# Window attention on one core: the bias of V moved to ScalarE, the image change cut anew, and TensorE's turn and spread set before the first row scores

## The chip, the cores and the metric

The kernel runs on one core of a Trainium2 chip. The time is that of the device, in microseconds, median over runs. The profile shows five engines: TensorE (PE, with its weight loads as PEld), VectorE (DVE), ScalarE (ACT), GpSimd (POOL) and SyncE (SP), which here only issues DMAs.

## The reference

The input x is 4 images of 128 channels, 112 by 112 pixels, float32. Each image is normalised in 32 groups of 4 channels, shifted by 3 pixels, projected to Q, K and V, cut into 256 windows of 7 by 7 pixels, and each window gets attention in 8 heads of 16 channels. The result is shifted back and added to x:

```python
y = group_norm(x, groups=32, eps=1e-5)
qkv = einsum('bchw,oc->bohw', roll(y, (-3, -3)), w_qkv) + b_qkv
# per window of 49 tokens and head of 16 channels:
attn = softmax(q @ k.T / sqrt(16)); o = attn @ v
out = x + roll(windows_back(o), (3, 3))
```

## The kernel before

Every engine has an instruction stream of its own, written out by hand, and semaphores tie them together. An image is 16 bands of 7 rows, a band is two groups of 8 windows (the second one wraps around the right edge, so its pixels are reached in three pieces instead of one), and the 4 images give 128 groups. Every engine has a function `step(g, ...)`, and in step g it works on several groups at once: the projections of g+1, the row scores of g, the column scores and exponentials of g-1, and sums, output and inverse of g-2. The groups are software pipelined, the order within a step is the order of the calls.

**TensorE**, step g: `project_v(g)` (L725), `sum_keys(g-2)` (L783), `weigh(g-2)` (L797), `project_q(g+1)` (L716), `row_scores(g, 0)` (L740), `turn_max(g-1)` (L752), `spread_inverse(g-2)` (L808), `column_scores(g-1)` (L765, and L772 for the part that subtracts the maximum), `row_scores(g, 1)` (L740), `project_k(g+1)` (L709). Row scores are only there to find each row's maximum. The turn transposes the negated maxima, the spread copies the inverse sums to all rows. `weigh` and `column_scores` share PSUM banks 6 and 7; turn, spread and V share bank 5.

**ScalarE**, step g: `evac_k(g)` (L356), `normalise(g+2)` (L349, `xn`, one or three pieces), `high_inverse(g-2)` (L384, `inv_hi`), `evac_even(g-2)` (L390, `even_out`), `evac_v(g)` (L379, `v_rows`), `evac_q(g+1)` (L361), `evac_neg(g-1)` (L368), two `exp(g-1)` (L373, `probs_t`).

**VectorE**, step g: `mask_q(g)` (L564), statistics of the next image in chunks of 448 pixels (L487, 28 chunks per image), `invert(g-2)` (L576, a reciprocal) and `low_inverse(g-2)` (L581), `join(g-2)` (L588, `summed`), `maximum(g, 0)` (L571), `low_q(g+1)` (L556), `scale_rows(g-2)` (L597, `mixed`), `maximum(g, 1)`. The join waits for `even_out`, and `column_scores` waits for the join. `change_image(b)` runs 6 steps, at b*32-8 to b*32-3, in which the statistics chunk is left out and the mean, variance and inverse root of the next image are worked out in small instructions, some ahead of `invert` and some between `low_inverse` and `join`. A Newton step for the root is L537 to L539; `gather_channels` is L507.

**POOL**, step g: `add_bias(g-3)` (L291), `split_max(g-1)`, `split_k(g)`, `add_image(g-3)` (L300, into `stage`), `split_x(g+2)`.

**SyncE** stores each band when both of its groups are in `stage`, and then loads the same band of the image after the next into the slot just freed (`load_band`, L201 and L202). So bands of images 2 and 3 arrive one by one while images 0 and 1 are stored. VectorE waits for them ahead of its statistics:

```python
for n in range(3):
    dve.wait_ge(loaded[b + 1], 32 * -(-(2 * n + 2) * STAT // BAND))
    two_steps(first + n, 2 * n, at)
dve.wait_ge(loaded[b + 1], 32 * BANDS)
```

Here `first` is b*16-1, so these are steps 30 to 35 for b = 1 and the last wait, for all 16 bands, stands ahead of step 36. The next two steps have two chunks each.

Of the kernel before, what the change touches and what calls it, by code (L numbers as in the profile page):

```python
# [6 lines left out]
B, C, H, W = 4, 128, 112, 112  # L7
# [5 lines left out]
BANDS = H // WS  # L13
# [22 lines left out]
def window_attention(nc, x, w_qkv, b_qkv, out):  # L36
# [7 lines left out]
    with ctx:  # L44
# [181 lines left out]
        def _(pool):  # L226
# [61 lines left out]
            def add_bias(g, half):  # L288
                pool.wait_ge(mixed_done, g + 2)
                pool.sem_inc(waited, 1)  # L290
                nc.gpsimd.tensor_scalar(mixed[:, half, :, :], mixed[:, half, :, :], bias[:, 2:3], None, ALU.add).then_inc(bias_added, 1)  # L291

# [12 lines left out]
            def step(g, n, par):  # L305
                if live(g - 3):
                    add_bias(g - 3, 1 - par)
                if live(g - 1):
                    split_max(g - 1, 1 - par)
                if live(g):  # L310
                    split_k(g, par)
                if live(g - 3):
                    add_image(g - 3, n - 2 + par, 1 - par)
                if live(g + 2):
                    split_x(g + 2, par)
# [12 lines left out]
        def _(act):  # L328
# [23 lines left out]

            def evac_k(g):
                act.wait_ge(k_mm, g + 1)
                wait(act, k_split, g)
                nc.scalar.activation(k32[:, :], psum[:, QK_BANK, 0:GT], ACT.Identity, bias=k_bias[:, 0:1]).then_inc(k_evac, 1)  # L356
# [35 lines left out]
            def step(g, n, par, b=0):  # L392
                if live(g):
                    evac_k(g)
                if live(g + 2):
                    normalise(g + 2, n + 1, par, b)
                if live(g - 2):
                    high_inverse(g - 2)
                if live(g - 2):
                    evac_even(g - 2)  # L400
                if live(g):
                    evac_v(g, par)
                if live(g + 1):
                    evac_q(g + 1)
                if live(g - 1):
                    evac_neg(g - 1)
                if live(g - 1):
                    exp(g - 1, 0)
                    exp(g - 1, 1)
# [14 lines left out]
            for g in range(GROUPS - 2, GROUPS + 2):  # L424
                step(g, g // 2, g & 1)

        @block.vector
        def _(dve):
# [87 lines left out]
            def group_mean():  # L516

                link(nc.vector.tensor_reduce(g_sum[:, :], grouped(mean_row), AX.X, ALU.add))
                link(nc.vector.scalar_tensor_tensor(grouped(work_a), g_sum[:, :, None].broadcast_to([C, 8, PER]), -1.0 / PER,
                                                    grouped(mean_row), ALU.mult, ALU.add))  # L520
                link(nc.vector.tensor_tensor(work_b[:, :], work_a[:, :], work_a[:, :], ALU.mult))

            def group_variance():

                link(nc.vector.tensor_tensor(work_a[:, :], work_b[:, :], var_row[:, :], ALU.add))
                link(nc.vector.tensor_reduce(g_var[:, :], grouped(work_a), AX.X, ALU.add))
                link(nc.vector.tensor_scalar(g_var[:, :], g_var[:, :], 1.0 / PER, EPS, ALU.mult, ALU.add))

            def guess_root():

                link(nc.vector.tensor_scalar(half_bits[:, :], g_var[:, :].bitcast(i32), 1, None, ALU.logical_shift_right))
                link(nc.vector.tensor_scalar(rs[:, :].bitcast(i32), half_bits[:, :], -1.0, float(0x5F3759DF), ALU.mult, ALU.add))

            def refine_root(steps):

                for _ in range(steps):
                    link(nc.vector.tensor_tensor(rs_t[:, :], rs[:, :], rs[:, :], ALU.mult))  # L537
                    link(nc.vector.scalar_tensor_tensor(rs_t[:, :], rs_t[:, :], -0.5, g_var[:, :], ALU.mult, ALU.mult))
                    link(nc.vector.scalar_tensor_tensor(rs[:, :], rs_t[:, :], 1.5, rs[:, :], ALU.add, ALU.mult))  # L539

            def scatter_groups():

                nc.vector.tensor_scalar(grouped(mean_row), g_sum[:, :, None].broadcast_to([C, 8, PER]), 1.0 / PER, None, ALU.mult)
                link(nc.vector.tensor_scalar(grouped(var_row), rs[:, :, None].broadcast_to([C, 8, PER]), X_SCALE, None, ALU.mult))

            def offer(b):

                wait(dve, xn_ready, (b - 1) * 2 * BANDS)
                nc.vector.transpose(mean_c[:, :], mean_row[:, :])
                link(nc.vector.transpose(rstd_c[:, b % 2, :], var_row[:, :]))  # L550
                nc.vector.scalar_tensor_tensor(shift_c[:, b % 2:b % 2 + 1], mean_c[:, 0:1], -1.0, rstd_c[:, b % 2, 0:1], ALU.mult,  # L551
                                               ALU.mult).then_inc(norm_ready, 1)

# [47 lines left out]
            def step(g, n, par, chunks=(), image_at=None, ahead=None, between=None):  # L601
# [11 lines left out]
                if between:  # L613
                    between()
# [16 lines left out]
            def change_image(b):  # L631

                g = (b * BANDS - 4) * 2
                for ahead, between in ((None, lambda: gather_channels(b)),
                                       (turn_channels, group_mean),
                                       (group_variance, guess_root),
                                       (lambda: refine_root(1), lambda: refine_root(1)),
                                       (lambda: refine_root(NEWTON - 2), scatter_groups),
                                       (None, lambda: offer(b))):
                    step(g, g // 2, g & 1, ahead=ahead, between=between)  # L640
                    g += 1
# [9 lines left out]
            gather_channels(0)  # L651
            turn_channels()
            group_mean()
            group_variance()
            guess_root()
            refine_root(NEWTON)
            scatter_groups()
            offer(0)
# [5 lines left out]
            step(2, 1, 0)  # L664
            step(3, 1, 1)
            with dve.Fori(2, BANDS - 4) as n:
                two_steps(n, 2 * n + 4, BANDS * BAND)
            for b in (1, 2):
# [3 lines left out]
                for n in range(3):  # L672
# [3 lines left out]
                for g in (2 * first + 6, 2 * first + 7):  # L676
                    chunk = 6 + 2 * (g & 1)
                    step(g, g // 2, g & 1, (chunk, chunk + 1), at)
                with dve.Fori(4, CHUNKS // 2 - 1) as n:
                    two_steps(n + first, 2 * n + 2, at)  # L680
# [10 lines left out]
        def _(pe):  # L691
# [120 lines left out]
            def step(g, par):  # L812
# [9 lines left out]
                if live(g):  # L822
                    row_scores(g, par, 0)
                if live(g - 1):
                    turn_max(g - 1, live(g))
                if live(g - 2):
                    spread_inverse(g - 2)
                if live(g - 1):
# [34 lines left out]
```

## Time and profile before

| | |
|---|---|
| median of 3 runs | 943.32 us (942.41 to 944.63) |
| the profiled execution | 941.08 us, its span 938.9 us |
| TensorE busy | 865.0 us, 92% of the span |
| VectorE busy | 766.3 us, 82% |
| POOL busy | 739.3 us, 79% |
| ScalarE busy | 665.1 us, 71% |
| mean granted TensorE clock | 0.99 |
| one ordinary step | 6.69 us |

Times are counted from the start of the span. A row of the timeline gives start, duration, engine, line, operation and tiles; "x3" behind it means three instructions of one kind merged; a bracket says how long the engine was idle before it and who ended that. Consecutive instructions of ScalarE and VectorE overlap a little, so the pitch from start to start can be shorter than the duration.

### The profile page before, as it was taken

The page shows a single profiled execution, that of the slowest core. Times are in us where ns is not written, and L with a number is a line of the kernel's source. Part 1 is how long each engine was busy: PE and PEld are TensorE (multiplying, and loading weights), DVE is VectorE, ACT ScalarE, POOL GpSimd, SP SyncE. Part 2 cuts the span into 40 slices and gives each one's busy share as a digit, 9 for nine tenths or more (in the row PEclk, how much of TensorE's full clock was granted, in tenths as well). Part 3 has the DMA queues.
Part 4 walks back from the last instruction along what each step waited for, and adds up shares of the span by engine and source line. Part 5 has one row for each costly group of instructions (what it writes and reads, how often), then busy time and mean ns, then how long its engine had stood idle before and what let it go on. Part 6 is the DMA issues. An engine that isn't in the chain of part 4 may idle for free. (4 is left out here: it accounts for less than half of the span.)

```text
span 938.9 us, 104445 instructions
## 1 busy us (share of the span) xinstructions
PE 865.0 (92%) x46473; PEld 708.7 (75%) x46473; DVE 766.3 (82%) x1399; ACT 665.1 (71%) x1297; POOL 739.3 (79%) x1191
## 2 busy tenths in 40 slices
PE   0479999998999999999999999999899999999994
PEld 0358888887788888887788888887678888888883
DVE  8657888889889888888888888888987777777873
ACT  2347777776677777777677777777677777777772
POOL 1347888887788888888788888888788888888883
PEclk9999999999999999999999999999999999999998
DMA  9401122112112211221211000000000000000001
GB/s 380 177 5 58 46 68 68 60 42 69 48 55 68 69 43 60 68 68 34 69 54 50 35 34 34 17 34 34 17 34 35 19 32 34 34 22 29 34 34 36
DMA packets 29912, 51.87 MB, mean 55 GB/s; under 512 B 3649, under 2 KB 28865, under 8 KB 29761
## 3 DMA queue, kind: packets, MB, share of 16 engines
q1 hardware_dynamic: 29888, 51.59, 15.8%
q8 instruction: 11, 0.18, 0.1%
q14 instruction: 13, 0.10, 0.0%
HBM read 25.89 MB, written 25.69 MB: 55 GB/s over the span
## 5 line engine op out<-in xcount | busy, mean ns | idle before, releaser
L373 ACT ACTIVATE probs_t<-psum,exp_scale 128x800 f32<-128x800 f32 x256 | 223.2, 923 | 139.6 <-PE psum L772 139.6
L571 DVE TENSOR_REDUCE neg_max<-psum 100x16 f32<-100x784 f32 x256 | 249.2, 974 | 39.1 <-PE psum L740 31.1
L291 POOL TENSOR_SCALAR mixed<-mixed,bias 128x392 f32<-128x392 f32 x128 | 161.7, 1263 | 123.2 <-DVE mixed L597 123.2
L740 PEld LDWEIGHTS psum<-k_hi,q_masks 32*128 32x128 f16 x8192 | 175.3, 91 | 46.3 <-issue 42.8
L740 PE MATMUL psum<-k_hi,q_masks 32*128 32x49 f16 x8192 | 197.8, 179 | 3.0 <-DVE neg_max L571 2.3
L740 PE MATMUL psum<-k_lo,q_masks 32*128 32x49 f16 x4096 | 182.6, 179 | 0.0
L740 PEld LDWEIGHTS psum<-k_lo,q_masks 32*128 32x128 f16 x4096 | 161.0, 91 | 0.0
L300 POOL TENSOR_TENSOR stage<-mixed,image 128x343 f32 (+7 forms) x256 | 144.2, 583 | 0.4 <-POOL mixed L291 0.4
L765 PE MATMUL psum<-q_masks,k_hi 32*64 32x100 f16 x8192 | 128.7, 219 | 16.1 <-DVE summed L588 13.3
L349 ACT ACTIVATE xn<-image,shift_c,rstd_c 128x21 f32 (+6 forms) x256 | 132.4, 573 | 8.0 <-DVE shift_c L551 6.1
L797 PE MATMUL psum<-probs_t,v_rows 64*32 64x100 f32 x8192 | 131.4, 252 | 2.4 <-issue 2.4
L783 PE MATMUL psum<-probs_t,sum_rows 128*32 128x49 f32 x8192 | 117.7, 209 | 9.6 <-ACT probs_t L373 2.7
L783 PEld LDWEIGHTS psum<-probs_t,sum_rows 128*32 128x32 f32 x8192 | 103.8, 110 | 28.5 <-issue 25.2
L275 POOL TENSOR_TENSOR k_lo<-k,k_hi 128x392 f16<-128x392 f32 x128 | 116.5, 910 | 10.7
L265 POOL TENSOR_TENSOR xn_lo<-xn,xn_hi 128x392 f16<-128x392 f32 x128 | 116.2, 908 | 10.7
L564 DVE TENSOR_SCALAR q_masks<-q_halves,even_odd 128x800 f16<-128x800 f16 x256 | 120.6, 511 | 2.3 <-DMA image<-in_x_dram 2.3
L765 PEld LDWEIGHTS psum<-q_masks,k_hi 32*64 32x64 f16 x8192 | 103.5, 102 | 22.5 <-issue 17.8
L765 PE MATMUL psum<-q_masks,k_lo 32*64 32x100 f16 x4096 | 111.7, 218 | 0.0
L797 PEld LDWEIGHTS psum<-probs_t,v_rows 64*32 64x32 f32 x8192 | 102.5, 106 | 11.4 <-issue 2.8
L588 DVE SCALAR_TENSOR_TENSOR summed<-psum,v_scale,even_out 128x392 f32<-128x392 f32 x128 | 80.1, 625 | 38.1 <-ACT even_out L390 37.4
L725 PE MATMUL psum<-w_lo,xn_hi 128*128 128x128 f16 x512 | 94.9, 222 | 0.0
L725 PE MATMUL psum<-w_hi,xn_lo 128*128 128x128 f16 x512 | 94.8, 222 | 0.0
(112 smaller groups left out, 1828.2 us busy)
## 6 DMA issues: line engine op xcount, KB each, us to landing
out_dram<-stage SPq DMA_DIRECT2D x64, 224.0 KB, 2.1
out_dram<-stage SPq DMA_DIRECT2D x64, 168.0 KB, 1.9
image<-in_x_dram SPq DMA_DIRECT2D x32, 224.0 KB, 2.6
image<-in_x_dram SPq DMA_DIRECT2D x1, 6104.0 KB, 28.2
image<-in_x_dram SPq DMA_DIRECT2D x34, 168.0 KB, 2.5
image<-in_x_dram SPq DMA_DIRECT2D x6, 896.0 KB, 9.2
image<-in_x_dram SPq DMA_DIRECT2D x1, 728.0 KB, 14.3
w_nat<-in_L_conv_w_qkv_dram SPq DMA_DIRECT2D x1, 192.0 KB, 2.4
```

What stands on the lines that cost most here:

```text
L275: nc.gpsimd.tensor_tensor(k_lo[:, par, :, 0:TOK], k, k_hi[:, par, :, 0:TOK], ALU.subtract).then_inc(k_split, 1)
L291: nc.gpsimd.tensor_scalar(mixed[:, half, :, :], mixed[:, half, :, :], bias[:, 2:3], None, ALU.add).then_inc(bias_added, 1)
L300: last = nc.gpsimd.tensor_tensor(pixel_view(stage[:, bass.ds(st, BAND)], piece), token_view(mixed[:, half, :, :], piece), pixel_view(image ...
L349: last = nc.scalar.activation(token_view(xn, piece), pixel_view(image[:, bass.ds(at, BAND)], piece), ACT.Identity, bias=shift_c[:, b % 2:b ...
L373: nc.scalar.activation(probs_t[:, 2 * u:2 * u + 2, :, :].rearrange("p h a q -> p h (a q)"), psum[:, COL_BANKS[u], 0:PAIRS * ROWS2], ACT.Ex ...
L564: last = nc.vector.tensor_scalar(both[:, :, e, :], q_halves[:, :, :, :].rearrange("p l w q -> p (l w) q"), even_odd[:, e:e + 1], None, ALU ...
L571: nc.vector.tensor_reduce(neg_max[:, par, 2 * j:2 * j + 2, :], psum[0:ROWS2, ROW_BANKS, 0:GT] .rearrange("p h (w k) -> p h w k", k=TOK), A ...
L725: last = nc.tensor.matmul(psum[:, V_BANK, a * C:(a + 1) * C], xs[:, par, 2 * a:2 * a + 2, :].rearrange("p w k -> p (w k)"), wv[:, 2, :], s ...
L740: last = nc.tensor.matmul(psum[:, ROW_BANKS.start + h - 2 * j, w * TOK:(w + 1) * TOK], q_masks[rows, par, low + w * ROWS2:low + w * ROWS2 ...
L765: nc.tensor.matmul(psum[side, COL_BANKS[h // 2].start + h % 2, a * ROWS2:(a + 1) * ROWS2], k[rows, par, w, :], q_masks[rows, par, low + w ...
L783: last = nc.tensor.matmul(psum[c * PC:(c + 1) * PC, SUM_BANK, SPARE_SUM], sum_rows[:, a, e, :, :, :].rearrange("p t w s -> p (t w s)"), pr ...
L797: last = nc.tensor.matmul(psum[c * PC:(c + 1) * PC, OUT_BANKS.start + s, a * C:a * C + ROWS2], v_rows[side, par, a, c * PC:(c + 1) * PC], ...
```

## The change

Four edits go together. `add_bias` leaves POOL and becomes an activation on ScalarE, behind `normalise` and ahead of `high_inverse`; ScalarE's last loop gets one step more for it. On ScalarE `evac_v` now stands before `evac_even`. VectorE's image change becomes a list of pieces, one per step and each ahead of `invert` (with three Newton steps it is eight entries), it starts two steps earlier, and the chunks of statistics are dealt out anew: steps 2 and 3 get one each, the steps behind an image change have two chunks from the third pair on, and the wait for all bands stands ahead of that third pair. TensorE issues `turn_max` and `spread_inverse` before `row_scores(g, par, 0)`.

```diff
@@ gpsimd
-            def add_bias(g, half):
-                pool.wait_ge(mixed_done, g + 2)
-                pool.sem_inc(waited, 1)
-                nc.gpsimd.tensor_scalar(mixed[:, half, :, :], mixed[:, half, :, :], bias[:, 2:3], None, ALU.add).then_inc(bias_added, 1)
...
             def step(g, n, par):
-                if live(g - 3):
-                    add_bias(g - 3, 1 - par)
@@ scalar
+            def add_bias(g, half):
+                act.wait_ge(mixed_done, g + 2)
+                nc.scalar.activation(mixed[:, half, :, :], mixed[:, half, :, :], ACT.Identity, bias=bias[:, 2:3]).then_inc(bias_added, 1)
...
                     normalise(g + 2, n + 1, par, b)
+                if live(g - 3):
+                    add_bias(g - 3, 1 - par)
                 if live(g - 2):
                     high_inverse(g - 2)
+                if live(g):
+                    evac_v(g, par)
                 if live(g - 2):
                     evac_even(g - 2)
-                if live(g):
-                    evac_v(g, par)
...
-            for g in range(GROUPS - 2, GROUPS + 2):
+            for g in range(GROUPS - 2, GROUPS + 3):
@@ vector
+            def norm_steps(b):
+                return [lambda: gather_channels(b), turn_channels, group_mean, group_variance] + NEWTON * [refine_root] + [lambda: offer(b)]
...
             def change_image(b):
-                g = (b * BANDS - 4) * 2
-                for ahead, between in ((None, lambda: gather_channels(b)),
-                                       (turn_channels, group_mean),
-                                       (group_variance, guess_root),
-                                       (lambda: refine_root(1), lambda: refine_root(1)),
-                                       (lambda: refine_root(NEWTON - 2), scatter_groups),
-                                       (None, lambda: offer(b))):
-                    step(g, g // 2, g & 1, ahead=ahead, between=between)
-                    g += 1
+                first = (b * BANDS - 5) * 2
+                for g, piece in enumerate(norm_steps(b), first):
+                    step(g, g // 2, g & 1, ahead=piece)
...
-            step(2, 1, 0)
-            step(3, 1, 1)
-            with dve.Fori(2, BANDS - 4) as n:
-                two_steps(n, 2 * n + 4, BANDS * BAND)
+            step(2, 1, 0, (8,), BANDS * BAND)
+            step(3, 1, 1, (9,), BANDS * BAND)
+            with dve.Fori(2, BANDS - 5) as n:
+                two_steps(n, 2 * n + 6, BANDS * BAND)
...
-                for n in range(3):
+                for n in range(2):
                     dve.wait_ge(loaded[b + 1], 32 * -(-(2 * n + 2) * STAT // BAND))
                     two_steps(first + n, 2 * n, at)
                 dve.wait_ge(loaded[b + 1], 32 * BANDS)
-                for g in (2 * first + 6, 2 * first + 7):
-                    chunk = 6 + 2 * (g & 1)
-                    step(g, g // 2, g & 1, (chunk, chunk + 1), at)
-                with dve.Fori(4, CHUNKS // 2 - 1) as n:
-                    two_steps(n + first, 2 * n + 2, at)
+                for n in (2, 3):
+                    for par in range(2):
+                        chunk = 4 * (n - 1) + 2 * par
+                        step(2 * (first + n) + par, first + n, par, (chunk, chunk + 1), at)
+                with dve.Fori(4, CHUNKS // 2 - 2) as n:
+                    two_steps(n + first, 2 * n + 4, at)
@@ tensor
                     project_q(g + 1, 1 - par)
-                if live(g):
-                    row_scores(g, par, 0)
                 if live(g - 1):
                     turn_max(g - 1, live(g))
                 if live(g - 2):
                     spread_inverse(g - 2)
+                if live(g):
+                    row_scores(g, par, 0)
                 if live(g - 1):
                     column_scores(g - 1, 1 - par)
```

The addition of variance and squared deviation moves from `group_variance` into `group_mean`, the first guess of the root from a function of its own into `group_variance`, and `scatter_groups` into `offer`. The instructions themselves are the same.

## Rows read from the trace of the kernel before

**Rows 1.** The page's first part: busy time, share and instructions of the engines.

```profile
PE 865.0 (92%) x46473; PEld 708.7 (75%) x46473; DVE 766.3 (82%) x1399; ACT 665.1 (71%) x1297; POOL 739.3 (79%) x1191
```

**Rows 2.** The timeline of ScalarE in an odd step (start, us, engine, line).

```profile
504.50 1.74 ACT L373 ACTIVATE probs_t<-psum,exp_scale 128x800 f32<-128x800 f32 x2 [0.95 <-PE psum L772]
...
506.60 1.31 ACT L349 ACTIVATE xn<-image,shift_c,rstd_c 128x343 f32 x3
507.86 0.24 ACT L384 CAST inv_hi<-inv 128x49 f16<-128x49 f32 x1
508.28 0.59 ACT L390 ACTIVATE even_out<-psum,v_scale 128x392 f32<-128x392 f32 x1 [0.19 <-PE psum L797]
508.77 0.58 ACT L379 COPY v_rows<-psum 128x512 f32<-128x512 f32 x1
...
511.19 1.74 ACT L373 ACTIVATE probs_t<-psum,exp_scale 128x800 f32<-128x800 f32 x2 [0.95 <-PE psum L772]
```

**Rows 3.** The timeline of VectorE: a join, masks of step 34, a late join.

```profile
508.90 0.63 DVE L588 SCALAR_TENSOR_TENSOR summed<-psum,v_scale,even_out 128x392 f32<-128x392 f32 x1 [0.32 <-ACT even_out L390]
...
278.93 0.95 DVE L564 TENSOR_SCALAR q_masks<-q_halves,even_odd 128x800 f16<-128x800 f16 x2
...
241.58 0.63 DVE L588 SCALAR_TENSOR_TENSOR summed<-psum,v_scale,even_out 128x392 f32<-128x392 f32 x1
```

**Rows 4.** The timeline of TensorE from Q to the column scores.

```profile
501.84 0.33 PE L716 MATMUL psum<-xn_hi,w_lo 128*128 128x392 f16 x1
...
502.10 0.20 PE L740 MATMUL psum<-k_hi,q_masks 32*128 32x49 f16 x2
...
502.81 0.22 PE L752 MATMUL psum<-ident,neg_halves 100*128 100x100 bf16 x1
...
503.15 0.25 PE L765 MATMUL psum<-q_masks,k_hi 32*64 32x100 f16 x8
...
242.35 0.25 PE L765 MATMUL psum<-q_masks,k_hi 32*64 32x100 f16 x8 [0.40 <-DVE summed L588]
```

**Rows 5.** The page's costliest groups: busy and mean ns, idle before, its releaser.

```profile
L291 POOL TENSOR_SCALAR mixed<-mixed,bias 128x392 f32<-128x392 f32 x128 | 161.7, 1263 | 123.2 <-DVE mixed L597 123.2
```

**Rows 6.** The timeline of ScalarE in an even step, step 34.

```profile
277.45 1.74 ACT L373 ACTIVATE probs_t<-psum,exp_scale 128x800 f32<-128x800 f32 x2 [0.95 <-PE psum L772]
...
279.56 0.75 ACT L349 ACTIVATE xn<-image,shift_c,rstd_c 128x392 f32 x1
280.90 0.24 ACT L384 CAST inv_hi<-inv 128x49 f16<-128x49 f32 x1 [0.59 <-DVE inv L576]
```

**Rows 7.** The timeline of ScalarE in a step with two chunks.

```profile
515.15 0.24 ACT L384 CAST inv_hi<-inv 128x49 f16<-128x49 f32 x1 [1.10 <-DVE inv L576]
515.29 0.58 ACT L390 ACTIVATE even_out<-psum,v_scale 128x392 f32<-128x392 f32 x1
...
518.17 1.74 ACT L373 ACTIVATE probs_t<-psum,exp_scale 128x800 f32<-128x800 f32 x2 [0.95 <-PE psum L772]
```

**Rows 8.** ScalarE's timeline: exponentials at both ends of an image change.

```profile
205.64 1.75 ACT L373 ACTIVATE probs_t<-psum,exp_scale 128x800 f32<-128x800 f32 x2 [0.95 <-PE psum L772]
...
250.69 1.74 ACT L373 ACTIVATE probs_t<-psum,exp_scale 128x800 f32<-128x800 f32 x2 [1.26 <-PE psum L772]
```

**Rows 9.** VectorE's timeline: first instruction of a Newton step and its follower.

```profile
230.11 0.20 DVE L537 TENSOR_TENSOR rs_t<-rs 128x8 f32<-128x8 f32 x1
...
231.03 0.47 DVE L576 RECIPROCAL inv<-psum 128x49 f32<-128x49 f32 x1
```

**Rows 10.** SyncE's timeline: the last part of image 2's last band.

```profile
284.96 0.35 SPq L202 DMA_DIRECT2D image<-in_x_dram  x1
```

**Rows 11.** Line L202 alone: time from its DMAs to their landing.

```profile
DMA to landing us min/median/max: 2.4/2.5/3.1
```

**Rows 12.** The windows view: busy times, granted clock, DMA, behind a change's waits.

```profile
455.60:459.10 3.50, 3.50 (x90) 2.82 (x79) 2.88 (x8) 2.77 (x4) 2.14 (x4) 0.54 0.01 2
```

More of the change, by code:

```diff
@@ L521, in group_mean, with refine_root, offer @@
                 link(nc.vector.tensor_tensor(work_b[:, :], work_a[:, :], work_a[:, :], ALU.mult))
+                link(nc.vector.tensor_tensor(work_a[:, :], work_b[:, :], var_row[:, :], ALU.add))
             def group_variance():
-                link(nc.vector.tensor_tensor(work_a[:, :], work_b[:, :], var_row[:, :], ALU.add))
                 link(nc.vector.tensor_reduce(g_var[:, :], grouped(work_a), AX.X, ALU.add))
                 link(nc.vector.tensor_scalar(g_var[:, :], g_var[:, :], 1.0 / PER, EPS, ALU.mult, ALU.add))
-            def guess_root():
                 link(nc.vector.tensor_scalar(half_bits[:, :], g_var[:, :].bitcast(i32), 1, None, ALU.logical_shift_right))
                 link(nc.vector.tensor_scalar(rs[:, :].bitcast(i32), half_bits[:, :], -1.0, float(0x5F3759DF), ALU.mult, ALU.add))
[L534 to L541, printed above, removed]
+            def refine_root():
+                link(nc.vector.tensor_tensor(rs_t[:, :], rs[:, :], rs[:, :], ALU.mult))
+                link(nc.vector.scalar_tensor_tensor(rs_t[:, :], rs_t[:, :], -0.5, g_var[:, :], ALU.mult, ALU.mult))
+                link(nc.vector.scalar_tensor_tensor(rs[:, :], rs_t[:, :], 1.5, rs[:, :], ALU.add, ALU.mult))
+            def offer(b):
+                wait(dve, xn_ready, (b - 1) * 2 * BANDS)
                 nc.vector.tensor_scalar(grouped(mean_row), g_sum[:, :, None].broadcast_to([C, 8, PER]), 1.0 / PER, None, ALU.mult)
                 link(nc.vector.tensor_scalar(grouped(var_row), rs[:, :, None].broadcast_to([C, 8, PER]), X_SCALE, None, ALU.mult))
-            def offer(b):
-                wait(dve, xn_ready, (b - 1) * 2 * BANDS)
                 nc.vector.transpose(mean_c[:, :], mean_row[:, :])
@@ L599, in scale_rows, with step @@
                                         summed[:, :, :].rearrange("p (s a) q -> p s a q", s=2), ALU.mult).then_inc(mixed_done, 1)
-            def step(g, n, par, chunks=(), image_at=None, ahead=None, between=None):
+            def step(g, n, par, chunks=(), image_at=None, ahead=None):
                 if live(g):
@@ L612, in step @@
                     low_inverse(g - 2)
-                if between:
-                    between()
                 if live(g - 2):
@@ L650, in _ @@
                     take_stats(chunk * STAT, chunk)
[L651 to L658, printed above, removed]
+            for piece in norm_steps(0):
+                piece()
             work_out_scales()
```

## The prediction

> **What bounds the kernel now.** I read the busy line of the page first. TensorE is busy for 92% of the span [rows 1], and no other engine is above 82%, so a change on another engine counts only where TensorE waits for it. Then I laid the timelines of ScalarE, VectorE and TensorE for one step beside each other. From one first exponential (the start of `exp(g-1, 0)`) to the next is 504.50 to 511.19, so 6.69 us a step [rows 2]. I call the start of that first exponential T and give all other moments as T plus so much, because the chain goes round in it: the exponentials feed `sum_keys` and `weigh` of the next step, behind these come Q, the row scores and the column scores, and the column scores release the next exponential.
>
> In an odd step ScalarE starts `xn` at T+2.10, `inv_hi` at T+3.36, `even_out` at T+3.78 and `v_rows` at T+4.27 [rows 2]. VectorE starts the join (L588) at T+4.40 [rows 3]. `column_scores` waits for that join, since `weigh` left its result in banks 6 and 7. How tight is it? Where the join does come last, it ends at 241.58 + 0.63 = 242.21 and the column scores start at 242.35 [rows 3, 4], a lag of 0.14. From the start of the column scores to the next exponential is 503.15 to 504.50 = 1.35 [rows 2, 4]. So a join that starts at J allows the next exponential at J + 0.63 + 0.14 + 1.35 = J + 2.12. Now J is T+4.40, which allows T+6.52, and the step takes 6.69: the slack is 0.17 us. That number decides most of what follows.
>
> **The change part by part.**
>
> TensorE order. Now there are three changes of matmul shape between Q and the column scores: Q (128x128) to row scores (32x128), row scores to turn and spread (128x128), these to the column scores (32x64). The first costs 0.10: the last Q matmul starts at 501.84, streams its 392 columns in about 0.16 (its neighbours' pitch is 0.17), and the row scores start at 502.10 [rows 4]. After it there are two: Q and turn share a shape. One gap of 0.09 to 0.10 goes, and I take 0.09 of each of 128 steps, 11.5 us at the very most, if nothing else waits. The trace of before has no direct step from 32x128 to 32x64; if that were free, the saving would be 0.19 a step. The Trainium skill, TensorEngine Tiling (Array Packing), Key Properties, says that changing the tiling mode drains TensorE; by it one of three drains goes, and the gap of 0.10 agrees.
>
> What is paid: `turn_max` waits for `v_rows` of this step. From the turn to the next exponential is then 0.34 (turn, spread and a gap: 502.81 to 503.15), 0.71 (row scores and a gap: 502.10 to 502.81) and 1.35: 2.40 [rows 2, 4].
>
> ScalarE. POOL loses an instruction of 1.263 us [rows 5], but POOL idles before it and its first reader waits for nothing of it, so that saves nothing on the path. ScalarE gains an activation over 392 columns. It has no such one from SBUF with a bias alone; the nearest rows are `even_out`, 0.59 long and 0.49 in pitch to the next [rows 2], and `xn` in one piece, 0.75 [rows 6], a pitch of about 0.64. I take 0.49 and keep 0.64 for the range. It stands ahead of `inv_hi`, and behind it `v_rows` now goes ahead of `even_out`, another 0.49. `inv_hi` to its successor is 0.14 when that is ready [rows 7]; `even_out` to the join is 0.62 [rows 2, 3].
>
> - Odd step (three pieces of `xn`): `inv_hi` T+3.36+0.49 = 3.85, `v_rows` 3.99, `even_out` 4.48, join 5.10, next exponential 7.22. Against 6.69 that is +0.53. The turn's own chain gives less: `v_rows` ends at 4.57, turn about 4.67, plus 2.40 = 7.07.
> - Even step: `xn` starts at T+2.11 in one piece of 0.75 [rows 6], so the bias fits before `inv_hi`, which waits for the reciprocal until T+3.45 (277.45 to 280.90). `v_rows` 3.59, `even_out` 4.08, join 4.70, next exponential 6.82: +0.13.
>
> Mean +0.33. This holds with one chunk of statistics in the step or none (odd steps are ScalarE's in both). Ordinary steps: 4 to 21, 30 to 33 and 38 to 53, 62 to 65 and 70 to 85, and the last image, 34 less the drain of the pipeline: about 90. 90 x 0.33 = 29.7 us.
>
> Steps with two chunks. There `inv_hi` comes at 515.15 - 511.19 = T+3.96, and the step takes 6.98 to the exponential at 518.17 [rows 2, 7]. After: 3.96 + 0.14 + 0.49 + 0.62 + 2.12 = 7.33. The change makes four of them per image (34 to 37) out of two. Leaving the first aside: 3 x 7.33 - (6.69 + 2 x 6.98) = +1.3, for two images +2.6.
>
> The image change. Six steps take 205.64 to 250.69 = 45.05 [rows 8], with the two ordinary ones that the eight pieces now also use, 58.43. A piece now stands ahead of the reciprocal and takes the place of a chunk of about 0.54, with nothing between inverse and join. A Newton step takes 230.11 to 231.03 = 0.92 [rows 9], so `inv_hi` at 3.45 + 0.38 = 3.83 and the step 7.20; the odd floor is 7.22. The two widest pieces (aggregate, and the mean with an addition more) I put at 7.2 and 7.7. Eight steps then sum to about 58.3. That is a gain over the old 7.5 us a step, given back by the two steps more and by ScalarE: 0 us, with 2 either way per image.
>
> The wait for the next image, moved by the same edit. Two-step pairs 15 and 16 (steps 30 to 33) now come before `dve.wait_ge(loaded[b+1], 32 * BANDS)`, not three pairs, so VectorE meets it at the start of step 34 (and 66). But band 15 of image b+1 is only loaded after band 15 of image b-1 is stored, and that one is finished by POOL's `add_image(31)` inside step 34. The second half of that load is issued at 284.96 [rows 10]. T of that step is 277.45 and VectorE starts its masks at 278.93 = T+1.48 [rows 3, 6]. So the issue is at T+7.51, and the landing takes 2.5 us at the median [rows 11]. POOL without the bias is some 0.2 earlier, so VectorE goes on at about T+9.8, not T+1.48: it stands for 8.3 us. Today it meets the wait at step 36, 13.4 later, when all has landed. Queued behind it are masks, statistics, reciprocal, join and both maxima. From masks to `inv_hi` in a two-chunk step is 3.96 - 1.48 = 2.48, and from `inv_hi` to the exponential 3.37, so the next T is 9.8 + 5.85 = 15.65, +8.96 over 6.69. Nothing covers it: TensorE stops at the turn. Twice: 17.9 us. POOL and SyncE need nothing of VectorE's step 34 for that store and load, so it is a stall and not a deadlock.
>
> The clock. Behind the waits of the second image change the granted clock was 0.54 over 3.5 us [rows 12]. That is 1.2 GHz of its two levels nearly throughout. TensorE idle for almost 9 us should bring the same: a stretch of 3.4 us at half rate costs at most 1.7, two cost 3.4, and partly covered one next to nothing. I take 1.5 per stall, 3 in all. The Trainium skill, TensorE: Matmul & The Clock Gate, Part 1, has the clock halved after idleness; without any such fall the sum would be 3 us less.
>
> Sum: 29.7 + 2.6 + 0 + 17.9 + 3 = 53.2. The profiled execution took 941.1, so 994.3; it lies 2.2 under the median of the runs shown, 943.3, so **996 us**.
>
> **The rivals.**
>
> - A, the forecast: ScalarE's chain and the load wait both bind. 996.
> - B, only the load wait binds: the bias and the swap hide in ScalarE's idle time (0.95 us before the exponentials [rows 2]). Against: that idle time lies behind the join, not ahead of it. 943.3 + 17.9 + 3 + 2.6, less up to 8 for the gap saved in 90 steps: 959 to 967.
> - C, only ScalarE's chain binds, since the loads are in time. Against: the issue at 284.96 stands 6.0 behind the masks. 943.3 + 29.7 + 2.6 = 976.
> - D, faster: the gap saved decides. It does if `even_out` still starts by T+3.95 (3.78 + 0.17) and `v_rows` ends before Q does, T+4.2, and the load costs under the saving. 0.09 x 128 = 11.5: 932; with the second gap free too, 920. Against: both conditions are missed in odd steps by 0.5 and 0.4.
> - E, worse: the bias has a pitch of 0.64 (+0.15 in 45 odd steps, 7), the clock stays down longer (to 3.4 per stall, 4 more), the mean piece is slowed by POOL. 1003 to 1012.
>
> **How the numbers follow.** A 0.72, B 0.08, C 0.06, D 0.03, E 0.09, and 0.02 for cancelling terms that leave no change. A alone spans 984 to 1003 (mean step +0.25 to +0.38, clock 0 to 6). Leaving out D, part of B and the top of E gives 966 to 1008. Within 0.2% is about what a measurement of this kernel cannot tell from no change: faster 0.03, same 0.02, slower 0.95.
>
> **What would show it.** Ordinary steps that alternate near 6.8 and 7.2 instead of 6.69; TensorE waiting ahead of L752 for `v_rows` or ahead of the column scores for the join in nearly every odd step; ScalarE idle less than 0.95 before the exponentials only if I am wrong on what is late. Two waits of VectorE's masks for the image load of about 8 us, at steps 34 and 66, and the granted clock down behind each. Eight change steps of 7.2 to 7.7 with none near 8.6. I am wrong if steps stay at 6.6 to 6.7 (then the bias was covered), or if VectorE passes the load wait without stopping.

## The result and the profile after

The changed kernel takes **1001.07 us** (median of 4 runs, 1000.26 to 1001.44), against 943.39 for the kernel before in the same series: a ratio of 1.0609, interval 1.0591 to 1.0628. It is 6% slower; the prediction was 996, in a range of 966 to 1008. The profiled span grew from 938.9 to 998.5 us. The page's first part and one of its costliest groups:

```profile
PE 883.4 (88%) x46473; PEld 716.9 (72%) x46473; DVE 732.6 (73%) x1399; ACT 706.9 (71%) x1425; POOL 600.3 (60%) x1063
...
L559 DVE TENSOR_SCALAR q_masks<-q_halves,even_odd 128x800 f16<-128x800 f16 x256 | 97.7, 424 | 19.1 <-DMA image<-in_x_dram 19.1
```

Against [rows 1] POOL lost 139 us and ScalarE gained 42, yet TensorE's share fell to 88%. VectorE's masks (L559) now wait 19.1 us for the image load. The rest of the loss is in no single wait. Cut at the first exponentials of the steps, the 59.6 us are:

| stretch | before | after less before | predicted |
|---|---|---|---|
| 89 ordinary steps | 595.6 | +36.8 | +29.4 |
| steps 34, 35, 66, 67 | 26.8 | +23.2 | +22.2 |
| steps 36, 37, 68, 69 | 28.0 | +1.4 | +1.4 |
| three image changes, 27 steps | 196.2 | -3.2 | 0 |
| head, steps 2 to 4, end | 92.3 | +1.4 | 0 |

An odd step takes 7.16 to 7.17 us and an even one 7.06, in place of 6.69 for both. ScalarE's timeline, an even step and then an odd one:

```profile
497.96 1.74 ACT L370 ACTIVATE probs_t<-psum,exp_scale 128x800 f32<-128x800 f32 x2 [1.54 <-PE psum L754]
...
500.06 0.76 ACT L342 ACTIVATE xn<-image,shift_c,rstd_c 128x392 f32 x1
500.70 0.63 ACT L348 ACTIVATE mixed<-mixed,bias 128x392 f32<-128x392 f32 x1
501.39 0.24 ACT L381 CAST inv_hi<-inv 128x49 f16<-128x49 f32 x1
501.80 0.58 ACT L376 COPY v_rows<-psum 128x512 f32<-128x512 f32 x1 [0.17 <-PE psum L779]
502.28 0.59 ACT L387 ACTIVATE even_out<-psum,v_scale 128x392 f32<-128x392 f32 x1
...
505.01 1.74 ACT L370 ACTIVATE probs_t<-psum,exp_scale 128x800 f32<-128x800 f32 x2 [1.53 <-PE psum L754]
506.65 0.59 ACT L353 ACTIVATE k<-psum,k_bias 128x392 f32<-128x392 f32 x1
507.12 1.32 ACT L342 ACTIVATE xn<-image,shift_c,rstd_c 128x343 f32 x3
508.32 0.62 ACT L348 ACTIVATE mixed<-mixed,bias 128x392 f32<-128x392 f32 x1
508.83 0.23 ACT L381 CAST inv_hi<-inv 128x49 f16<-128x49 f32 x1
508.96 0.59 ACT L376 COPY v_rows<-psum 128x512 f32<-128x512 f32 x1
509.43 0.60 ACT L387 ACTIVATE even_out<-psum,v_scale 128x392 f32<-128x392 f32 x1
...
512.18 0.93 ACT L370 ACTIVATE probs_t<-psum,exp_scale 128x800 f32<-128x800 f32 x1 [1.54 <-PE psum L754]
```

In the odd step nothing between `xn` and `even_out` waits: it is one queue, and `even_out` starts at T+4.42 where it was T+3.78 [rows 2]. In the even step there is one wait, that of `v_rows` for L779, which is `weigh`: after its `inv_hi` there are 0.41 us to `v_rows` and not 0.13. That wait is the prediction's gap (below). ScalarE's idle time before the exponentials rose from 0.95 to 1.5, so its own load is not what is short; the place of each instruction in the queue is.

The joins that close both steps, and the turn of the even one (VectorE's and TensorE's timelines):

```profile
502.90 0.62 DVE L583 SCALAR_TENSOR_TENSOR summed<-psum,v_scale,even_out 128x392 f32<-128x392 f32 x1 [0.74 <-ACT even_out L387]
...
510.07 0.63 DVE L583 SCALAR_TENSOR_TENSOR summed<-psum,v_scale,even_out 128x392 f32<-128x392 f32 x1 [0.69 <-ACT even_out L387]
```

```profile
502.52 0.20 PE L734 MATMUL psum<-ident,neg_halves 100*128 100x100 bf16 x1 [0.21 <-ACT v_rows L376]
...
502.86 0.20 PE L722 MATMUL psum<-k_hi,q_masks 32*128 32x49 f16 x2
...
503.68 0.25 PE L747 MATMUL psum<-q_masks,k_hi 32*64 32x100 f16 x8
```

Join plus 2.12 gives 505.02 and 512.19; the exponentials start at 505.01 and 512.18. So the constant taken from before holds. The turn waits for `v_rows` in every step but one, as forecast, and row scores follow it by 0.34. From row scores to column scores are then 0.82 us, where 0.71 is enough [rows 4]: the column scores stand about 0.1 for the join, which ends at 503.52, 0.16 before they start. So the join sets the step, and the turn's chain would be ready 0.1 earlier. The profile names the join as what the column scores wait for in one step alone of this kernel; what bears the reading out is `c_swap_only` (below), where a join at the same T+4.95 gives the same step of 7.06 and the profile names it in 126 steps.

Step 34, VectorE and ScalarE, and the windows view around it (us, busy time and instructions by engine, granted clock, DMA share, GB/s):

```profile
287.82 0.97 DVE L566 TENSOR_REDUCE neg_max<-psum 100x16 f32<-100x784 f32 x1
297.23 0.77 DVE L559 TENSOR_SCALAR q_masks<-q_halves,even_odd 128x800 f16<-128x800 f16 x2 [8.44 <-DMA image<-in_x_dram]
```

```profile
287.23 1.74 ACT L370 ACTIVATE probs_t<-psum,exp_scale 128x800 f32<-128x800 f32 x2 [1.54 <-PE psum L754]
...
299.54 0.24 ACT L381 CAST inv_hi<-inv 128x49 f16<-128x49 f32 x1 [8.94 <-DVE inv L571]
...
303.76 1.75 ACT L370 ACTIVATE probs_t<-psum,exp_scale 128x800 f32<-128x800 f32 x2 [2.41 <-PE psum L754]
```

```profile
278.00:292.00 14.00, 13.09 (x717) 10.61 (x717) 8.97 (x15) 9.52 (x19) 9.10 (x17) 1.00 0.18 57
292.00:307.00 15.00, 6.60 (x232) 5.61 (x232) 7.33 (x15) 4.72 (x10) 2.84 (x8) 0.55 0.16 54
307.00:320.00 13.00, 12.15 (x700) 9.89 (x701) 10.61 (x18) 8.62 (x20) 8.31 (x14) 0.99 0.08 27
```

The masks wait 8.44 us, until T+10.00 (T+9.8 predicted); the step takes 16.53 and the next 8.46. The granted clock, 1.00 before, is 0.55 over the next 15 us, nearly all at 1.2 GHz, and comes back after that.

### The profile page after: what moved, and what is told of

It reads as the page before. It is cut to its first block, busy times and chain, and to the rows that moved or that the text cites. A ratio compares the mean times of both kernels' runs of the same rounds, so it can differ in the third digit from the quotient of the medians.

```text
span 998.5 us, 104360 instructions
## 1 busy us (share of the span) xinstructions
PE 883.4 (88%) x46473; PEld 716.9 (72%) x46473; DVE 732.6 (73%) x1399; ACT 706.9 (71%) x1425; POOL 600.3 (60%) x1063
## 4 chain that ended last, share of the span: by engine, by line
PE 53%; ACT 22%; issue 14%; DVE 5%; DMA 3%; ACTq 1%; SPq 1%; POOL 0%; POOLq 0%; DVEq 0%
PE psum L722 13%; PE psum L747 12%; ACT xn L342 8%; ACT v_rows L376 7%; PE psum L779 6%; PE psum L765 5%; PE psum L707 4%; PE psum L691 4%; PE psum L754 4%; DMA image<-in_x_dram 3%; ACT probs_t L370 3%; PE psum L790 3%; PE psum L734 3%; ACT mixed L348 2%; ACT k L353 1%
## 5 line engine op out<-in xcount | busy, mean ns | idle before, releaser
L282 POOL TENSOR_SCALAR neg_halves<-neg_max 100x32 bf16<-100x32 f32 x128 | 61.9, 483 | 297.9 <-DVE neg_max L566 297.9
L779 PE MATMUL psum<-probs_t,v_rows 64*32 64x100 f32 x8192 | 131.1, 252 | 2.0 <-issue 2.0
L765 PE MATMUL psum<-probs_t,sum_rows 128*32 128x49 f32 x8192 | 117.8, 209 | 10.3 <-ACT probs_t L370 2.7
L747 PEld LDWEIGHTS psum<-q_masks,k_hi 32*64 32x64 f16 x8192 | 107.5, 103 | 17.9 <-issue 3.3
L747 PE MATMUL psum<-q_masks,k_lo 32*64 32x100 f16 x4096 | 114.5, 219 | 0.0
L559 DVE TENSOR_SCALAR q_masks<-q_halves,even_odd 128x800 f16<-128x800 f16 x256 | 97.7, 424 | 19.1 <-DMA image<-in_x_dram 19.1
L779 PEld LDWEIGHTS psum<-probs_t,v_rows 64*32 64x32 f32 x8192 | 102.4, 106 | 10.9 <-issue 2.3
L576 DVE SCALAR_TENSOR_TENSOR inv_rows<-inv_hi,low_rows,inv 128x49 f16<-128x49 f16 x128 | 49.1, 384 | 70.6 <-ACT inv_hi L381 70.6
```

Of the source, the lines that this page charges most:

```text
L559: last = nc.vector.tensor_scalar(both[:, :, e, :], q_halves[:, :, :, :].rearrange("p l w q -> p (l w) q"), even_odd[:, e:e + 1], None, ALU ...
L747: nc.tensor.matmul(psum[side, COL_BANKS[h // 2].start + h % 2, a * ROWS2:(a + 1) * ROWS2], k[rows, par, w, :], q_masks[rows, par, low + w ...
L765: last = nc.tensor.matmul(psum[c * PC:(c + 1) * PC, SUM_BANK, SPARE_SUM], sum_rows[:, a, e, :, :, :].rearrange("p t w s -> p (t w s)"), pr ...
L779: last = nc.tensor.matmul(psum[c * PC:(c + 1) * PC, OUT_BANKS.start + s, a * C:a * C + ROWS2], v_rows[side, par, a, c * PC:(c + 1) * PC], ...
```

## The experiments

Each was compared with the kernel before on the same chip (medians 941.1 to 941.7). Step times are from first exponential to first exponential, and the columns "ordinary", "34/35, 66/67" and "changes" below are the rows of the table above: the difference from the kernel before, summed, in us.

### The load wait, and the order on ScalarE

`a_load_in_time` is the changed kernel with that wait where it costs nothing:

```diff
-                dve.wait_ge(loaded[b + 1], 32 * BANDS)
                 for n in (2, 3):
                     for par in range(2):
...
+                    dve.wait_ge(loaded[b + 1], 32 * (5 if n == 2 else BANDS))
```

(one wait per pair: step 34 waits for five bands, step 36 for all.)

> The changed kernel with one edit: ahead of the third pair of steps behind an image change VectorE waits for 5 bands, which is what chunks 4 to 7 need, and for all 16 only ahead of the fourth pair. Theory (the early wait costs on its own): the exponential-to-exponential time of step 34 falls from 16.53 to about 7.5 and that of step 35 from 8.46 to 7.5, so 10 us per image, 20 us in all: about 981. No masks wait for an image load but the first. Rival (the stall only takes up time that the steps would lose anyway, since ScalarE's chain is late): the gain stays under 10 us, above 991.

Measured: 978.55, ratio 1.0389 (1.0364 to 1.0415), span 976.4. In the page:

```profile
L559 DVE TENSOR_SCALAR q_masks<-q_halves,even_odd 128x800 f16<-128x800 f16 x256 | 97.9, 425 | 2.0 <-DMA image<-in_x_dram 2.0
```

The wait fell from 19.1 to 2.0 us and the span by 22.1. Steps 34 to 37 take 7.45, 7.16, 7.45, 7.16. Ordinary steps are unchanged, 7.17 and 7.06: +36.8 us stays. So the two causes are separate, and neither is the whole.

`b_vector_only` is the kernel before with VectorE's part of the change alone, `b_vector_load_in_time` that with the edit above, and `b_bias_only` the kernel before with the bias alone moved to ScalarE, in the place the change gives it:

```diff
@@ scalar
                     normalise(g + 2, n + 1, par, b)
+                if live(g - 3):
+                    add_bias(g - 3, 1 - par)
                 if live(g - 2):
                     high_inverse(g - 2)
```

> The kernel before with VectorE's part of the change alone (the image change in eight one-step pieces, the chunks dealt anew, the wait for all bands ahead of the third pair). Theory: two stalls of about 8.7 us over a step plus 2.2 us of clock each cost 22; the pieces, all ahead of the reciprocal, give back, because with even_out ahead of v_rows a piece of 0.92 gives 3.45+0.38+0.14+0.62+2.12 = 6.71 a step, so eight steps of some 6.8 against 58.4 us now, 4 us per image change, 12 in all: 943 + 22 - 12 = 953. Rival (the pieces gain nothing, as I put it in the prediction): 965. Rival (no stall without ScalarE's late chain): 932.

> The kernel before with VectorE's part of the change, and with the wait for all bands moved back to the fourth pair (5 bands ahead of the third). Theory: only the gain of the pieces is left, about 12 us: 931 to 933, faster than before. Rival (pieces gain nothing on their own): 943.

> The kernel before with only the bias of V moved from POOL to ScalarE, between xn and inv_hi. Theory (the slack ahead of the join covers nearly all of it): odd steps have inv_hi at T+3.87, even_out at 4.01, join at 4.63, next exponential 6.75, even steps stay at 6.69, so +0.06 in 64 steps, 4 us: 947. Rival (the bias costs its full 0.5 us in odd steps): 975. Rival (POOL's relief speeds VectorE up): under 942.

| | median | ratio (95%) | ordinary | 34/35, 66/67 | changes |
|---|---|---|---|---|---|
| b_vector_only | 951.47 | 1.0099 (1.0075 to 1.0123) | +0.4 | +20.1 | -8.2 |
| b_vector_load_in_time | 933.32 | 0.9908 (0.9882 to 0.9935) | +0.1 | +1.2 | -8.2 |
| b_bias_only | 943.99 | 1.0022 (1.0005 to 1.0038) | +6.7 | +0.3 | -1.1 |

The early wait costs 18 us here and 22 in the changed kernel. The pieces by themselves gain 2.7 us per image change: with the old ScalarE order the eight steps end at 6.7 to 7.0, with one of 7.73, where the old ones reached 8.59. With the wait in time this version is 0.9% faster than before, the only one in the study that is. The bias alone makes odd steps 6.83 (6.75 expected; `v_rows` ends later too, and the turn waits for it in its old place) and leaves even ones at 6.69, which is 0.2% in sum. Since this bias costs ScalarE 0.5 us in both orders, the 0.4 us a step of the change is to be looked for in the swap and the turn.

### Swap and turn, one at a time

`c_swap_only` puts `evac_v` ahead of `evac_even` in the kernel before, `c_turn_only` puts turn and spread ahead of the first row scores, `c_turn_swap` does both:

```diff
@@ scalar (c_swap_only, c_turn_swap)
+                if live(g):
+                    evac_v(g, par)
                 if live(g - 2):
                     evac_even(g - 2)
-                if live(g):
-                    evac_v(g, par)
@@ tensor (c_turn_only, c_turn_swap)
-                if live(g):
-                    row_scores(g, par, 0)
                 if live(g - 1):
                     turn_max(g - 1, live(g))
                 if live(g - 2):
                     spread_inverse(g - 2)
+                if live(g):
+                    row_scores(g, par, 0)
```

> The kernel before with v_rows ahead of even_out on ScalarE and nothing else. Theory (the join's chain): both now wait for the end of weigh, so v_rows starts at T+3.85, even_out at 4.33, the join at 4.95, and the next exponential comes at 7.07 in odd and even steps alike, +0.38 in some 110 steps: 984. Rival (ScalarE's idle 0.95 us ahead of the exponentials takes it up): 943. Rival (only the place of the turn makes the order matter): 943 too, and the two kernels with the turn moved would carry the loss.

> The kernel before with turn and spread ahead of the first row scores on TensorE and nothing else. Theory: the turn waits for v_rows, which ends at T+4.85 behind even_out; turn 4.98, next exponential 2.49 later at 7.47, +0.78 in some 115 steps: about 1030. Rival (the turn's wait is covered and one shape change fewer counts): 932. Rival (the turn costs no more than the swap does): 985.

> The kernel before with both, the bias still on POOL. Theory: v_rows from 3.85 to 4.43, turn 4.56, by this chain 7.05; join 4.95, by that one 7.07: as the swap alone, 984, and 45 us less than the turn alone. So on top of the turn the swap is a gain, on top of the old order a loss. Rival (the two costs add up): 1070.

| | median | ratio (95%) | odd, even step |
|---|---|---|---|
| c_swap_only | 981.88 | 1.0412 (1.0369 to 1.0455) | 7.06, 7.06 |
| c_turn_only | 1032.43 | 1.0948 (1.0902 to 1.0995) | 7.64, 7.37 |
| c_turn_swap | 1020.51 | 1.082 (1.0779 to 1.0862) | 7.64, 7.15 |

The swap alone costs about as much as the whole change without its stall (981.9 and 978.6): 7.06 in every ordinary step, although the bias is off ScalarE and TensorE keeps its old order. ScalarE's timeline of it has the same wait as the changed kernel:

```profile
500.58 0.58 ACT L379 COPY v_rows<-psum 128x512 f32<-128x512 f32 x1 [0.23 <-PE psum L797]
501.06 0.59 ACT L390 ACTIVATE even_out<-psum,v_scale 128x392 f32<-128x392 f32 x1
...
503.80 1.75 ACT L373 ACTIVATE probs_t<-psum,exp_scale 128x800 f32<-128x800 f32 x2 [1.32 <-PE psum L772]
```

`v_rows` waits for `weigh` (L797), `even_out` queues 0.48 behind it, and 0.62 + 2.12 later comes the exponential: 503.80, as it should. With the turn moved and the bias on ScalarE as well (`d_turn_swap_bias`, below) odd steps rise from 7.06 to 7.17 and even ones stay, so on top of the swap this bias costs at most 0.1 us, in every second step.

The turn costs more alone than in company, and `c_turn_swap` missed its expected 984 by 36 us. The reason is on POOL. Its timeline in an odd step, with VectorE's of the same stretch behind it:

```profile
605.92 2.48 POOL L291 TENSOR_SCALAR mixed<-mixed,bias 128x392 f32<-128x392 f32 x1 [0.72 <-DVE mixed L597]
...
609.54 0.91 POOL L275 TENSOR_TENSOR k_lo<-k,k_hi 128x392 f16<-128x392 f32 x1
```

```profile
605.15 0.56 DVE L597 TENSOR_TENSOR mixed<-psum,summed 128x392 f32<-128x392 f32 x1
...
606.50 0.76 DVE L564 TENSOR_SCALAR q_masks<-q_halves,even_odd 128x800 f16<-128x800 f16 x2
607.18 0.62 DVE L487 BATCH_NORM_STATS2 stats<-image  x1
```

```profile
610.55 0.20 PE L740 MATMUL psum<-k_hi,q_masks 32*128 32x49 f16 x2 [0.62 <-issue]
```

The bias takes 2.48 us, not 1.26. `k_lo` queues behind it on POOL and ends at 610.45, and the row scores that read it start at 610.55 (last fence, TensorE), after 0.62 us of idleness. The instruction is the same. In the kernel before (POOL, then VectorE) the masks come later in it and are themselves the slower ones:

```profile
505.11 1.26 POOL L291 TENSOR_SCALAR mixed<-mixed,bias 128x392 f32<-128x392 f32 x1 [0.56 <-DVE mixed L597]
```

```profile
505.98 0.94 DVE L564 TENSOR_SCALAR q_masks<-q_halves,even_odd 128x800 f16<-128x800 f16 x2
```

There they start 0.87 us after the bias, with 0.39 of it left; here 0.58 after it. The bias took 1.26 us in every step of the kernel before; in `c_turn_swap` it takes 2.48 in ordinary odd steps and 1.71 in even ones (2.474 at the median of all). Both lengths are the same in the last image, where VectorE has no statistics to take, so the statistics beside it have no part in this. The Trainium skill, GPSIMD Engine Reference, 1. Specifications, says that GpSimd's SBUF interfaces are shared with VectorE and contended by some of VectorE's instructions; the trace agrees, with 1.26 and 2.48 us for the one instruction.

`d_turn_swap_bias` tests whether the bias on POOL is what makes the row scores late: the changed kernel with VectorE's part of the kernel before, so turn, swap and the bias off POOL.

```diff
@@ the changed kernel, @@ vector
-                for g, piece in enumerate(norm_steps(b), first):
-                    step(g, g // 2, g & 1, ahead=piece)
+                for ahead, between in ((None, lambda: gather_channels(b)),
...
+                    step(g, g // 2, g & 1, ahead=ahead, between=between)
```

> The kernel before with the turn moved, the swap, and the bias on ScalarE, VectorE's part left as it was. Theory (in the kernel with turn and swap alone POOL's bias, stretched from 1.26 to as much as 2.48 us where it meets VectorE's masks, makes k_lo late for the row scores, and it is this that takes 7.64 in odd steps): with the bias off POOL odd steps fall to 7.17 and even ones stay at 7.06, about 987. Rival (POOL has no part in it, the bias on ScalarE only adds): 1020 or more.

Measured: 983.20, ratio 1.0453 (1.0427 to 1.0478), steps of 7.17 and 7.06 as in the changed kernel. So once the turn goes first, taking the bias off POOL is worth 37 us (1020.5 to 983.2), while against the old order it is worth nothing. The run takes the whole instruction off POOL and not only its longer time. That it is the longer time follows from the rows: `k_lo` ends 2.05 us behind the bias and 0.1 ahead of the row scores, so with a bias of 1.26 us it could end 1.2 earlier, and TensorE's wait ahead of them is 0.62.

### The bias behind the evacuations

If ScalarE's queue is too long ahead of `even_out`, the bias could stand behind it. `a_bias_late_in_time` does that in `a_load_in_time`, `best_bias_late` in `b_vector_load_in_time`. The edit of the first is shown; in the second the bias leaves POOL and stands at the same place, behind `evac_even` and `evac_v` in their old order:

```diff
@@ scalar
-                if live(g - 3):
-                    add_bias(g - 3, 1 - par)
                 if live(g - 2):
                     high_inverse(g - 2)
...
+                if live(g - 3):
+                    add_bias(g - 3, 1 - par)
                 if live(g + 1):
                     evac_q(g + 1)
```

> The changed kernel with the load in time (979) and with the bias behind even_out instead of ahead of inv_hi. Theory: v_rows cannot start before weigh ends at T+3.85; in odd steps the bias ahead of it makes that 3.95, and without it odd steps take 7.06 as the even ones do: 56 x 0.11 = 6 us, 973. Rival (the bias is what costs the most of the 0.42 a step): under 960. Rival (the later image addition on POOL or the later q and neg rows cost more): over 985.

> VectorE's part of the change with the load in time on the kernel before (933), and the bias on ScalarE behind v_rows, with even_out first and TensorE's order as before. Theory: the bias now stands where ScalarE has slack (q rows are read 0.6 later, neg rows 0.3 to 0.5 later than they are ready), so steps stay at 6.69, and POOL's relief shortens a change step or two: 930 to 933. Rival (q or neg rows become late): steps of 6.8 to 7.0, 945 to 965.

Measured: 1007.07, ratio 1.0709 (1.0677 to 1.0740), and 975.25, ratio 1.0359 (1.0335 to 1.0383). Both expectations missed, by 34 and some 43 us. Even steps of `best_bias_late` are 6.69 as hoped, odd ones 7.51. Its POOL and ScalarE:

```profile
505.64 1.28 POOL L295 TENSOR_TENSOR stage<-mixed,image 128x343 f32 x3 [1.77 <-ACT mixed L348]
506.88 0.53 POOL L263 TENSOR_SCALAR xn_hi<-xn 128x392 f16<-128x392 f32 x1
507.50 1.93 POOL L265 TENSOR_TENSOR xn_lo<-xn,xn_hi 128x392 f16<-128x392 f32 x1
```

```profile
509.55 1.31 ACT L342 ACTIVATE xn<-image,shift_c,rstd_c 128x343 f32 x3 [0.91 <-POOL xn_lo L265]
```

`add_image` waits 1.77 us for the late bias, the splits queue behind it, `xn_lo` now meets VectorE's masks (507.90) and takes 1.93 in place of 0.91, with statistics beside it or without, and the next `xn` stands 0.91 us for it. What sets the odd step is again `k_lo`, further back in POOL's queue (POOL, then TensorE):

```profile
510.52 0.91 POOL L275 TENSOR_TENSOR k_lo<-k,k_hi 128x392 f16<-128x392 f32 x1
```

```profile
511.52 0.20 PE L722 MATMUL psum<-k_hi,q_masks 32*128 32x49 f16 x2 [0.75 <-issue]
```

It ends at 511.43, and the row scores start 0.09 later, after 0.75 us of idleness; the join of that step, at 511.49, would allow the exponential 0.3 us earlier than it came (513.92). Both sums had asked what the bias holds up on ScalarE and not what waits for it on POOL; only the second rival of the first expectation (over 985) named the image addition.

### A direct test of the wait for `weigh`, and what swamped it

`a_v_rows_four` gives `v_rows` four slots in the changed kernel, so that `evac_v` waits for a `weigh` two groups older. Its slots need four steps in TensorE's loop body:

```diff
-                wait(act, out_mm, g - 1)
+                wait(act, out_mm, g - 3)
...
-            with pe.Fori(1, GROUPS // 2) as n:
-                step(2 * n, 0)
-                step(2 * n + 1, 1)
+            with pe.Fori(1, GROUPS // 4) as n:
+                for k in range(4):
+                    step(4 * n + k, k & 1, (k - 2) & 3)
```

> The changed kernel with four buffers of v_rows instead of two (TensorE's loop unrolled to four steps), so that v_rows no longer waits for weigh of the same step. Theory (this wait, which my prediction left out, is what lifts the even steps from the 6.82 predicted to 7.06): even steps fall to 6.80, as v_rows starts at T+3.58 and the join at 4.68, odd steps stay at 7.17, where v_rows is ready only at 3.95: 60 x 0.26 = 16 us, 985. Rival (the extra comes from the longer way from turn to exponential): no change, 1001.

Measured: 1634.78, ratio 1.7312 (1.7235 to 1.7389). That says nothing on `weigh`, so `g_unroll_only` makes the loop body four steps long in the kernel before and changes nothing else.

> The kernel before with TensorE's loop body written out for four steps instead of two, the same instructions in the same order. Theory (the kernel with four buffers of v_rows took 1635 us because of its doubled loop body, whose instructions were fetched again and again: 412 packets of the instruction queue against 11): about 1600, with some 400 such packets. Rival (the buffers or their addresses did it): 943.

Measured: 1629.37, ratio 1.7309 (1.7262 to 1.7357). The same factor without the four slots, so the body's length is the cause and the test of `weigh` is void. The page of `g_unroll_only`, its instruction queue and a costly group:

```profile
q8 instruction: 412, 6.75, 1.7%
...
L740 PEld LDWEIGHTS psum<-k_hi,q_masks 32*128 32x128 f16 x8192 | 214.7, 98 | 237.5 <-issue 235.8
```

## Why the prediction held, and where its terms did not

- **Direction and both causes: right.** The load wait and ScalarE's queue ahead of the join each bind, and each is shown by a run that takes it away or has it alone.
- **Odd steps: right, in part by luck.** 7.22 predicted, 7.17 measured. `inv_hi` came at T+3.82 (3.85), `v_rows` 3.95 (3.99), `even_out` 4.42 (4.48), the join 5.06 (5.10). But the sum took the bias at its full 0.49 and had nothing for the wait for `weigh` (next point). Worked out the same way, the swap alone would give 3.36 + 0.14 + 0.49 + 0.62 + 2.12 = 6.73; `c_swap_only` took 7.06, and the bias on top costs 0.1. The full pitch of the bias stood in for a wait that the sum did not have.
- **Even steps: the step that failed.** The prediction put `v_rows` at T+3.59, right behind `inv_hi`, and the step at 6.82. It came at T+3.84 and the step took 7.06. The swap does not only put 0.48 us ahead of `even_out`: `v_rows` overwrites the slot that `weigh(g-2)` reads, so it has the same releaser as `even_out` and can't use the time before it. In the old order `even_out` took the wait, as its bracket in [rows 2] shows, and `v_rows` followed. This is 0.24 in each of 43 even steps, 10.3 us; the 46 odd steps give 2.8 back, and the sum is near the 36.8 - 29.4 = 7.4 by which ordinary steps were missed. The waits of the two kernels show it; the direct test was void, so it rests on `c_swap_only` and the rows.
- **"That saves nothing on the path", of the bias off POOL: right for the old order, wrong as a general term.** `b_bias_only` is 0.2% slower; behind the early turn the same move is worth 37 us. The prediction added four edits as if each had its own price. Their single prices do not add up: swap and turn alone cost 40 and 91 us over their base, and the two together 79. The sum was made on the timeline with all four edits in it, so it did not need single prices. That it came within 5 us of the time is also luck: ordinary steps were 7.4 too low, and the image changes, put 3.2 too high, gave part of that back.
- **The bias' pitch:** 0.49 taken, 0.51 in the odd step above, duration 0.619 at the median over 128. The Trainium skill, ScalarE: Activation LUTs, What ACT_TABLE_LOAD costs, gives 280 ns plus 0.833 ns an element with such a bias, an estimate of 0.607; the trace agrees.
- **The gap between shapes:** from the turn to the row scores it is 0.34, as forecast. The 0.71 behind them can't be read from the changed kernel, where the join comes later (0.82). In the ordinary even steps of `c_turn_only`, where the turn sets the step, it starts at T+4.99 and the next exponential at 7.37: 2.38, for 2.40. There the direct step from 32x128 to 32x64 can be seen too, and it is not free: 0.11 us from the last row scores to the first column scores, as much as from row scores to turn in the kernel before. Whether 0.09 is saved ahead of the turn no run shows, since the turn waits for `v_rows`; it would lie on a chain that is not the last, and bring nothing.
- **The stall: right.** Load issued at T+7.44 (7.51 less 0.2), masks at T+10.00 (9.8), two stalls +23.2 with the step behind each (22.2).
- **The clock: mis-sized.** 1.5 per stall was taken. The forecast chain without it is 15.65 and took 16.53, the next 7.33 and took 8.46: 2.0. Against `a_load_in_time` (7.45 and 7.16, its masks at T+1.48 and so 8.52 earlier) it is 0.56 + 1.30, about 1.9 per stall, if all of it is the clock.
- **Steps with two chunks: the sum right, by luck.** 7.33 was put for each of steps 36 and 37; they took 7.52 and 7.16, and the two misses cancel.
- **The image change: mis-sized.** 0 against -3.2, within the 2 either way per image. The narrow pieces hide in full behind the queue of ScalarE: the widest step took 7.48, not 7.7, the others 7.06 to 7.17.
- **Rivals.** B (959 to 967) fell with `a_load_in_time`, C (976) is what that run gives, at 978.6. E began at 1003 and was not reached. D's saving appeared in no run: every kernel with the turn ahead is slower.

**Open:** how a `v_rows` that is free of `weigh` would do in an even step, and why POOL's instruction pays in the one position and VectorE's in the other, and more in odd steps than in even ones.

## What to carry to other kernels

Before an instruction is moved ahead of another in a queue, look up every wait of the one that goes first: if it has the same releaser as the one it passes, the move buys nothing, and whoever follows comes later by its length, less what slack there is (here 0.55 us at the join, of which 0.17 was slack). A wait that stands at a loop's seam for data that arrives by the kernel's own stores has a due time; find the issue of the last load in the trace before the loop is cut anew. Prices of single edits measured alone do not add on a pipelined ring of engines: time the combinations, and ask beside which of VectorE's operations each of POOL's will fall, and what is queued behind it.

## What the hardware showed that was not expected

- **TensorE's loop body.** Four steps in the body instead of two, the same instructions in the same order: 941.4 to 1629.4 us. The instruction queue moved 6.75 MB in 412 packets, where the kernel before has 0.18 MB in 11, TensorE's idle time ends in "issue", and the mean granted clock fell from 0.99 to 0.755. What of the 688 us is fetching and what the clock was not separated.
- **POOL beside VectorE.** One instruction on the same tiles took 1.26, 1.71 or 2.48 us (bias), 0.91 or 1.93 (`xn_lo`). The longer times came where VectorE's masks began 0.4 to 0.6 us behind its start, the shortest bias where they began at 0.87 and were themselves slowed.
- **The clock behind a stall.** TensorE was idle for 8.8 us in each stall. The granted clock stood at 1.2 GHz for about 14 us around the first and 10 around the second, part of it still in the idleness: TensorE worked at half clock for 6.8 and 6.5 us. [rows 12] had shown only a stretch of 3.5 us.
